# Delta rule: running sums of the log decays spread over the partitions by a DMA through DRAM instead of by matmuls

## The chip, the cores and the metric

The kernel runs on one core of one Trainium2 chip. The metric is the device time of one execution in microseconds (us). TensorE is called PE (its weight loads PEld), VectorE DVE, ScalarE ACT, GpSimdE POOL, SyncE SP. All data are float32, and a float32 matmul shows as two matmul records in the trace.

## The reference, cut to what is computed

The kernel computes four layers, each a token mixer and a feed-forward part, on an input of 8 sequences x 512 tokens x 128 channels. The change lies in the mixer of the last layer, a gated delta rule with 8 heads, keys of 128 and values of 32 channels:

```python
g = -jnp.exp(A_log)[None, None, :] * jax.nn.softplus(x @ Wa + dt_bias[None, None, :])
alpha = jnp.exp(g)
...
def step(state, inp):
    q_t, k_t, v_t, a_t, b_t = inp
    retained = jnp.einsum('bhvk,bhk->bhv', state, k_t)
    rk = retained[..., None] * k_t[:, :, None, :]
    vk = v_t[..., None] * k_t[:, :, None, :]
    state = a4 * (state - b4 * rk) + b4 * vk
    o_t = jnp.einsum('bhvk,bhk->bhv', state, q_t)
    return (state, o_t)
```

The kernel does this in chunks of 128 tokens. In a chunk, token t sees token s through exp(G_t - G_s), where G is the running sum of g from the chunk's start. So a 128 x 128 matrix of differences is needed for each head and chunk: G_t along a row, the same in all partitions, less G_s, one number for each partition.

## The kernel before, in words

`delta_rule` (L1833) works on 16 units (NU). A unit is one sequence and four of its eight heads; it has four chunks (NT) of 128 tokens, so there are 64 chunks. `all_units` writes the order of the work out by hand: `in_turn` counts turns, nine to a chunk (NI), 36 to a unit, and in each turn emits a step of `solve` (chunk n - 1 of the turn), of `make` (chunk n + 1), of `invert` (chunk n) and the pieces of preparation that `pieces_at` has put there for this and the next units. Each engine runs its own part of this list strictly in order, and waits on counting semaphores (`wait_ge`) for the others.

- `make`, part 0, in the first turn of nine, builds the decays of a chunk. PE: L2027, four matmuls, one a head. The stationary operand is g of the chunk's 128 tokens, one column repeated 128 times, the moving operand the triangle `upto3`; the result, in the PSUM bank `mk`, is G_t in every partition. DVE: L2313, four instructions, takes G_s (`gc`) from it and clips at zero, into D. Then ACT takes the exponential (L2221) and POOL masks it (L2184).
- `make`, part 1 (turn 3) and part 2 (turn 6): PE multiplies keys by queries and keys by keys (L2035, into `mk` again), DVE multiplies with D (L2318, L2323, L2326).
- `solve`, "state" (turn 0): for chunks behind the first of a unit PE applies the state (L2073, 16 records), DVE forms the right-hand side r (L2357, L2358, L2360) and scales the state (L2362). For the first chunk of a unit DVE only copies (L2353). "solve 0" (turn 1): PE, L2085, waits for r.
- `invert`: products of 32 x 32 tiles (L2042) between which ACT (L2231) or DVE (L2338, L2340) works. Its first product, in turn 1 too, waits for DVE's L2333 and L2335, which stand behind L2313 in DVE's order.
- Preparation: key taps, four accumulating matmuls a head over 512 tokens (L2133, two records each), queries (L2129), squares of the norms (POOL L2211, then PE L2141), transposes of the norms (L2145), values (L2118, L2119), small projections (L2112, in one boundary of four) and the layer norm's mean (L2106, in one of eight).
- "gate": PE forms G and the chunk's total as columns (L2152, L2153) for a whole unit at turn 6 of the unit before; DVE copies them at turn 12 (L2433 to L2436, counted as "gc"), and ACT exponentiates (L2274 to L2276). The PSUM bank is one of two that go round (`ring_bank`); `emptied` makes PE wait until the last reader of a bank is done.

SP has no work in this stage.

Of the kernel before, what the change touches and what calls it, by code (L numbers as in the profile page):

```python
# [16 lines left out]
F32 = mybir.dt.float32  # L17
U32 = mybir.dt.uint32
ALU = mybir.AluOpType
ACT = mybir.ActivationFunctionType  # L20
AX = mybir.AxisListType

C = 128
B = 8
# [87 lines left out]
def ts(i, n):  # L112
    return slice(i * n, (i + 1) * n)
# [1719 lines left out]
def delta_rule(k):  # L1833

    nc = k.nc
    TAPS, NH, NT = 4, 8, 4
    with ExitStack() as s:
# [16 lines left out]
        cv = k.sb("d_conv", [C, T], stack=s)[:]  # L1854
        S = k.sb("d_S", [C, NH, 32], stack=s)
        D = k.sb("d_D", [C, 2, 4, C], stack=s)
        A, Pm = (k.sb("d_" + n, [C, 6, 4, C], stack=s) for n in ("A", "P"))
        M = k.sb("d_M", [C, 4, 5, 4, 32], stack=s)
        A32, Y = (k.sb("d_" + n, [C, 4, 4, 32], stack=s) for n in ("A32", "Y"))
# [2 lines left out]
        P = [k.ps[:, i, :] for i in range(8)]  # L1862
        q = small

        pe, act, dve, pool, dma = k.stage("delta_start")
# [20 lines left out]
        for n in (1,):  # L1886
            pe, act, dve, pool, dma = k.stage(f"delta_taps{n}")
# [72 lines left out]
        def all_units(name):  # L1960
# [41 lines left out]
            def emptied(e, u, what, x):  # L2002


                n = ring[u, what, x] - 2
                if n < 0:
                    return
                v, was, y = order[n]
                on_dve = {("norm", 1): "nh", ("small", 0): "abread", ("gate", 2): "gc", ("out", 2): "x"}
                if (was, y) in on_dve:  # L2010
                    e.wait_ge(dve.steps, dve.at(f"u{v}" + on_dve[was, y]))
                else:
                    done = {"values": f"values{y}", "keys": f"keys{y}", "out": f"oT{y}", "norm": "nln"}[was]
                    e.wait_ge(act.steps, act.at(f"u{v}{done}"))

            with nc.Block() as block:
                @block.tensor
                def _(e):
                    def make(u, c, part):
                        n, g, t = chunk(u, c), u % 2, ts(c, C)  # L2020
                        if part == 0:
                            if c == 0:
                                e.wait_ge(dve.steps, dve.at(f"u{u}g"))
                            if (u, c) > (0, 0):
                                e.wait_ge(dve.steps, dve.at("A" + (chunk(u, c - 1) if c else chunk(u - 1, 3))))
                            for h in range(4):
                                ins = e.matmul(mk[:, ts(h, C)], q["g"][:, c, 4 * g + h:4 * g + h + 1].to_broadcast([C, C]), k.w["upto3"][:], start=True, stop=True)  # L2027
                            ins.then_inc(pe.steps, pe.did(f"gb{n}"))
                        else:
                            if c == 0 and part == 1:  # L2030
                                e.wait_ge(act.steps, act.at(f"u{u}run7"))
                            e.wait_ge(dve.steps, dve.at((f"d{n}", f"P{n}")[part - 1]))
                            for h in range(4):
                                H = 4 * (u % 3) + h
                                ins = e.matmul(mk[:, ts(h, C)], QK[:, 1, H, t], QK[:, part - 1, H, t], start=True, stop=True)  # L2035
                            ins.then_inc(pe.steps, pe.did((f"kq{n}", f"kk{n}")[part - 1]))
# [61 lines left out]
                    def prepare(u, what, x):  # L2098
# [48 lines left out]
                        elif what == "gate" and x == 2:  # L2147
# [2 lines left out]
                            emptied(e, u, "gate", 2)  # L2150
                            b = ring_bank(u, "gate", 2)
                            e.matmul(b[:, 0:16], k.w["upto3"][:], q["g"][:, :, hs], start=True, stop=True)  # L2152
                            e.matmul(b[:, 16:32], k.w["ones3"][:], q["g"][:, :, hs], start=True, stop=True).then_inc(pe.steps, pe.did(tag + "cum"))  # L2153
                        elif what == "keys":
                            emptied(e, u, "keys", x)
                            e.wait_ge(act.steps, act.at(tag + "run7"))
# [59 lines left out]
                def _(e):  # L2216
# [16 lines left out]
                    def prepare(u, what, x):  # L2233
# [29 lines left out]
                        elif what == "gate" and x == 0:  # L2263
# [5 lines left out]
                            e.activation(four("sp"), four("t"), ACT.Ln, bias=1.0).then_inc(act.steps, act.did(tag + "sp"))  # L2269
                            e.wait_ge(act.steps, act.n)  # L2270
                            e.activation(four("beta"), four("beta"), ACT.Exp, scale=-1.0).then_inc(act.steps, act.did(tag + "beta"))
                        elif what == "gate" and x == 4:
                            e.wait_ge(dve.steps, dve.at(tag + "gc"))
                            e.activation(four("ga"), four("gc"), ACT.Exp).then_inc(act.steps, act.did())  # L2274
# [26 lines left out]
                def _(e):  # L2301
# [3 lines left out]
                    def make(u, c, part):  # L2305
                        n, g = chunk(u, c), u % 2
                        a = (2 * c + g) % 6
                        if part == 0:
                            e.wait_ge(pe.steps, pe.at(f"gb{n}"))
                            if c == 0:  # L2310
                                e.wait_ge(dve.steps, dve.at(f"u{u}gc"))
                            for h in range(4):
                                e.tensor_scalar(D[:, g, h], mk[:, ts(h, C)], q["gc"][:, c, 4 * g + h:4 * g + h + 1], 0.0,  # L2313
                                                ALU.subtract, ALU.min).then_inc(dve.steps, dve.did(f"d{n}"))
                        elif part == 1:
                            e.wait_ge(pe.steps, pe.at(f"kq{n}"))
# [296 lines left out]
def build(nc, a, counts, upto=99, first=0):  # L2613
    k = Kernel(nc, counts)
    k.dram = a
    with k.stack:
        gate_rows = nc.dram_tensor("gate_rows", (8, B * T), F32).ap()
        h_rows = nc.dram_tensor("h_rows", (C, B, T), F32).ap()
        load_weights(k, a)
        if first <= 0:  # L2620
            with ExitStack() as s:
# [34 lines left out]
        with nc.Block() as block:  # L2656
            @block.sync
            def _(e):
                e.dma_start(a["out"], k.X[:]).then_inc(dma.steps, dma.did("out"))
                e.wait_ge(dma.steps, dma.at("out"))  # L2660
# [106 lines left out]
```

## Time and profile before

| | us |
|---|---|
| three runs | 4041.48, 4056.18, 4058.17 (median 4056.18) |
| span of the profiled execution | 4054.5 |
| PE busy | 3480.2 (86%) |
| DVE busy | 2420.3 (60%) |
| ACT busy | 1593.8 (39%) |
| POOL busy | 537.6 (13%) |

The delta rule's units run from about 2500 to 3964 us of the span. The page's own line on the whole span hides this stage: its engines there are read from the windows below. "PEclk" is the clock that TensorE was granted, as a share of 2.4 GHz; it is either 1.0 or 0.5 at any moment, and the share is a mean over the window. In a timeline a row is a run of like instructions, with the start of the first, the time from there to the end of the last, and in brackets how long the engine had been idle and who released it. Matmul ends are modelled and overlap the next start, so the time that a group holds PE is the distance between starts.

### The profile page before, as it was taken

The numbers are of one execution on the slowest core, as the hardware profiler recorded it, in microseconds if no ns is written. First come the engines' busy times: TensorE is split into PE (matmuls) and PEld (weight loads), VectorE is DVE, ScalarE is ACT, GpSimd is POOL, SyncE is SP. The second block draws the span as 40 slices with busy tenths as digits, with TensorE's granted clock in tenths as the row PEclk, the third lists the DMA queues.
The fourth block names the chain that finished last, engine by engine and source line by source line (L and its number), as shares of the span: only waits on it lengthen the run. The fifth ranks groups of instructions, "written<-read, shape, count | busy, mean of one in ns | idle before, by whom it ended". The sixth has DMA issues, their size and how long they took to land. (4 is left out here: it accounts for less than half of the span.)

```text
span 4054.5 us, 124079 instructions
## 1 busy us (share of the span) xinstructions
PE 3480.2 (86%) x55256; PEld 2205.5 (54%) x55256; DVE 2420.3 (60%) x6248; ACT 1593.8 (39%) x2941; POOL 537.6 (13%) x564
## 2 busy tenths in 40 slices
PE   3877777679999998899977796999999999999985
PEld 1326665225555555555556342666666666666672
DVE  3757776337777667767775112566666666666545
ACT  1653333345444444444320243444434344443323
POOL 1212222000000000000000000222222222222210
PEclk9896667789888888989765797999999999999967
DMA  2000000121111111111000001000000000000000
GB/s 88 0 0 1 1 1 1 43 72 51 47 39 36 41 36 44 41 44 34 13 3 3 16 0 44 2 3 3 3 2 2 3 3 3 3 3 3 2 3 23
DMA packets 37030, 77.12 MB, mean 19 GB/s; under 512 B 7696, under 2 KB 11153, under 8 KB 35473
## 3 DMA queue, kind: packets, MB, share of 16 engines
q1 hardware_dynamic: 36496, 69.17, 5.3%
q8 instruction: 437, 7.16, 0.7%
q14 instruction: 97, 0.79, 0.1%
HBM read 64.83 MB, written 4.33 MB: 17 GB/s over the span
## 5 line engine op out<-in xcount | busy, mean ns | idle before, releaser
L1366 PE MATMUL ps<-g_hs,g_fc 128*128 128x512 f32 x448 | 276.0, 701 | 40.9 <-ACT g_hidden L1488 22.0
L1488 ACT ACTIVATE g_hidden<-ps 128x512 f32<-128x512 f32 x224 | 133.3, 595 | 383.9 <-PE ps L1366 383.3
L2133 PE MATMUL ps<-d_hp,d_w_k 128*128 128x512 f32 x512 | 282.5, 638 | 0.0
L1257 PEld LDWEIGHTS ps<-g_Q,g_K 32*32 32x32 f32 x12288 | 193.8, 114 | 144.9 <-issue 57.3
L2211 POOL TENSOR_TENSOR d_sq<-d_QK 128x512 f32<-128x512 f32 x128 | 133.0, 1039 | 934.0 <-ACT d_QK L2262 772.7
L1257 PE MATMUL ps<-g_Q,g_K 32*32 32x32 f32 (+1 forms) x12288 | 225.1, 218 | 34.4 <-issue 10.1
L1380 PE MATMUL ps<-g_hidden,g_proj 128*128 128x512 f32 x448 | 243.0, 636 | 0.0
L2231 ACT ACTIVATE d_F<-ps 128x128 f32<-128x128 f32 x256 | 70.8, 276 | 352.9 <-PE ps L2042 349.6
L1225 POOL COPY g_xb<-X 128x512 f32<-128x512 f32 x8 | 7.3, 907 | 1232.4 <-DVE X L1686 1121.5
L2406 DVE SCALAR_TENSOR_TENSOR d_conv<-ps,w_conv_q,d_conv 128x511 f32<-128x511 f32 (+2 forms) x192 | 142.3, 741 | 34.2 <-ACT d_conv L2256 30.3
L1366 PEld LDWEIGHTS ps<-g_hs,g_fc 128*128 128x128 f32 x448 | 79.5, 210 | 149.1 <-ACT g_hidden L1488 80.5
L2189 POOL TENSOR_TENSOR d_M<-d_A,w_joins 128x128 f32<-128x128 f32 (+1 forms) x128 | 114.3, 912 | 346.3 <-ACT d_A L2225 346.3
L2042 PE MATMUL ps<-d_X,d_M 32*32 32x32 f32 x8192 | 123.2, 196 | 41.7 <-DVE d_X L2338 21.9
L1273 PE MATMUL ps<-g_V,g_KT 32*32 32x64 f32 x4096 | 136.7, 256 | 25.1 <-issue 5.4
L794 PE MATMUL ps<-att_kg,att_qx 32*128 32x96 f32 x1024 | 121.7, 355 | 41.9 <-DVE att_qx L708 27.4
L2035 PE MATMUL ps<-d_QK 128*128 128x128 f32 x1024 | 154.5, 296 | 0.0
L1380 PEld LDWEIGHTS ps<-g_hidden,g_proj 128*128 128x128 f32 x448 | 91.2, 207 | 113.5 <-issue 103.7
L2042 PEld LDWEIGHTS ps<-d_X,d_M 32*32 32x32 f32 x8192 | 95.7, 108 | 101.9 <-issue 66.0
L2365 DVE TENSOR_TENSOR d_r<-d_r,ps 32x128 f32<-32x128 f32 x192 | 55.0, 286 | 159.7 <-PE ps L2078 88.6
L1490 ACT ACTIVATE g_hidden<-g_hidden 128x512 f32<-128x512 f32 x224 | 141.1, 630 | 7.1
L794 PEld LDWEIGHTS ps<-att_kg,att_qx 32*128 32x128 f32 x1024 | 115.6, 255 | 50.9 <-DVE att_qx L708 29.5
L771 ACT ACTIVATE att_pt<-ps 96x512 f32<-96x512 f32 x128 | 75.1, 592 | 169.7 <-PE ps L811 168.6
(479 smaller groups left out, 7885.7 us busy)
## 6 DMA issues: line engine op xcount, KB each, us to landing
g_hs<-gate_rows SPq DMA_DIRECT2D x56, 256.0 KB, 3.6
g_fc<-in_c_fc_dram SPq DMA_DIRECT2D x56, 256.0 KB, 4.1
g_proj<-in_c_proj_dram SPq DMA_DIRECT2D x56, 256.0 KB, 2.8
X<-in_x_dram SPq DMA_DIRECT2D x1, 2048.0 KB, 11.0
w_c_fc<-in_c_fc_dram SPq DMA_DIRECT2D x1, 2048.0 KB, 8.0
w_c_proj<-in_c_proj_dram SPq DMA_DIRECT2D x1, 2048.0 KB, 12.4
ex_root<-gate_rows SPq DMA_DIRECT2D x1, 2048.0 KB, 15.0
h_rows<-k SPq DMA_DIRECT2D x1, 2048.0 KB, 6.3
```

Of the source, the lines that this page charges most:

```text
L794: ins = e.matmul(scored[:, g, b], qx[ts(g, 32), q, 4 * u + b, :, :].rearrange("p h q -> p (h q)"), kg[ts(g, 32), q, 4 * u + b, :], start=T ...
L1257: ins = e.matmul(later(scored, n_), keys_, queries(n_, planes, r_, 4 * i + j), start=(turn_ == 0 and part == 0 and n_ != 1), stop=(part == 1),
L1273: ins = e.matmul(P[1][ts(h4, 32), 256 + j * 64:320 + j * 64], KT[rows, (KR, KI)[part], i, ts(h4, 32)], V[rows, i, 4 * c["sg"] + h4, (slice ...
L1366: e.matmul(P[2], fc[:, n % 2, ts(f, C)], hs[:, n % 2], start=True, stop=True).then_inc(pe.steps, pe.did(now(f"u{i}")))
L1380: e.matmul(P[3], proj[:, n % 2, f, :], r[:, (16 * c["half"] + i) % 5], start=(c["half"] == 0 and i == 0), stop=(c["half"] == 1 and i == 15 ...
L1488: e.activation(r[:, slot], P[2], ACT.Relu).then_inc(act.steps, act.did(now(f"r{i}")))
L1490: e.activation(r[:, slot], r[:, slot], ACT.Square).then_inc(act.steps, act.did(now(f"q{i}")))
L2035: ins = e.matmul(mk[:, ts(h, C)], QK[:, 1, H, t], QK[:, part - 1, H, t], start=True, stop=True)
L2042: ins = e.matmul(inv[rows, h], stationary[rows, h], moving[rows, h], start=True, stop=True, tile_position=(32 * j, 32 * j))
L2133: ins = e.matmul(b, w_k[:, j, ts(H, C)], hp_of(u)[:, j:j + T], start=(j == 0), stop=(j == TAPS - 1))
L2211: e.tensor_tensor(squares(x), qk, qk, ALU.mult).then_inc(pool.steps, pool.did(f"{tag}sq{x}"))
L2406: e.scalar_tensor_tensor(cv[:, late:], tap_bank(run)[:, 0:T - late], k.w["conv_q"][:, 4 * g + run // 2, 3 - late:4 - late], cv[:, late:], ...
```

## The change

PE's four matmuls of part 0 are gone from each chunk. For a whole unit, four matmuls with a stationary operand of 4 columns (the four heads' g) form G as rows, four partitions for each chunk, at partitions 0, 32, 64 and 96 of the bank that already holds the gate sums. ACT copies them to SBUF in turn 12 (four instructions), SP writes them to DRAM in four DMAs of 2 KB, waits, waits until DVE has read the last chunk of the unit before, and reads the 8 KB back into each of 128 partitions (`wide_rows`, 1 MB). DVE's part 0 then reads SBUF instead of the PSUM bank. PE's key-query matmuls wait for the last chunk's A instead of for DVE's differences.

```diff
--- before.py
+++ after.py
@@ -1854,6 +1854,8 @@
         cv = k.sb("d_conv", [C, T], stack=s)[:]
         S = k.sb("d_S", [C, NH, 32], stack=s)
         D = k.sb("d_D", [C, 2, 4, C], stack=s)
+        row4 = k.sb("d_decay_rows", [C, C], stack=s)
+        wide_rows = k.sb("d_wide_rows", [C, 4, 4, C], stack=s)
         A, Pm = (k.sb("d_" + n, [C, 6, 4, C], stack=s) for n in ("A", "P"))
         M = k.sb("d_M", [C, 4, 5, 4, 32], stack=s)
         A32, Y = (k.sb("d_" + n, [C, 4, 4, 32], stack=s) for n in ("A32", "Y"))
@@ -2007,6 +2009,8 @@
                     return
                 v, was, y = order[n]
                 on_dve = {("norm", 1): "nh", ("small", 0): "abread", ("gate", 2): "gc", ("out", 2): "x"}
+                if (was, y) == ("gate", 2):
+                    e.wait_ge(act.steps, act.at(f"u{v}rows"))
                 if (was, y) in on_dve:
                     e.wait_ge(dve.steps, dve.at(f"u{v}" + on_dve[was, y]))
                 else:
@@ -2014,22 +2018,30 @@
                     e.wait_ge(act.steps, act.at(f"u{v}{done}"))
 
             with nc.Block() as block:
+                @block.sync
+                def _(e):
+                    for u in range(NU):
+                        e.wait_ge(act.steps, act.at(f"u{u}rows"))
+                        for j in range(NT):
+                            e.dma_start(k.gc_rows[u, ts(j, 4), :], row4[32 * j:32 * j + 4, :]).then_inc(dma.steps, dma.did(f"u{u}rows"))
+                        e.wait_ge(dma.steps, dma.at(f"u{u}rows"))
+                        if u:
+                            e.wait_ge(dve.steps, dve.at(f"d{chunk(u - 1, 3)}"))
+                        src = k.gc_rows[u:u + 1].rearrange("a r t -> a (r t)")
+                        e.dma_start(wide_rows[:].rearrange("p i h t -> p (i h t)"), src.to_broadcast([C, 16 * C])).then_inc(dma.steps, dma.did(f"u{u}wide"))
+                        e.wait_ge(dma.steps, dma.at(f"u{u}wide"))
+
                 @block.tensor
                 def _(e):
                     def make(u, c, part):
                         n, g, t = chunk(u, c), u % 2, ts(c, C)
-                        if part == 0:
-                            if c == 0:
-                                e.wait_ge(dve.steps, dve.at(f"u{u}g"))
-                            if (u, c) > (0, 0):
-                                e.wait_ge(dve.steps, dve.at("A" + (chunk(u, c - 1) if c else chunk(u - 1, 3))))
-                            for h in range(4):
-                                ins = e.matmul(mk[:, ts(h, C)], q["g"][:, c, 4 * g + h:4 * g + h + 1].to_broadcast([C, C]), k.w["upto3"][:], start=True, stop=True)
-                            ins.then_inc(pe.steps, pe.did(f"gb{n}"))
-                        else:
+                        if part:
                             if c == 0 and part == 1:
                                 e.wait_ge(act.steps, act.at(f"u{u}run7"))
-                            e.wait_ge(dve.steps, dve.at((f"d{n}", f"P{n}")[part - 1]))
+                            if part == 2:
+                                e.wait_ge(dve.steps, dve.at(f"P{n}"))
+                            elif (u, c) > (0, 0):
+                                e.wait_ge(dve.steps, dve.at("A" + (chunk(u, c - 1) if c else chunk(u - 1, 3))))
                             for h in range(4):
                                 H = 4 * (u % 3) + h
                                 ins = e.matmul(mk[:, ts(h, C)], QK[:, 1, H, t], QK[:, part - 1, H, t], start=True, stop=True)
@@ -2150,7 +2162,10 @@
                             emptied(e, u, "gate", 2)
                             b = ring_bank(u, "gate", 2)
                             e.matmul(b[:, 0:16], k.w["upto3"][:], q["g"][:, :, hs], start=True, stop=True)
-                            e.matmul(b[:, 16:32], k.w["ones3"][:], q["g"][:, :, hs], start=True, stop=True).then_inc(pe.steps, pe.did(tag + "cum"))
+                            e.matmul(b[:, 16:32], k.w["ones3"][:], q["g"][:, :, hs], start=True, stop=True)
+                            for j in range(NT):
+                                ins = e.matmul(b[32 * j:32 * j + 4, 128:256], q["g"][:, j, hs], k.w["upto3"][:], start=True, stop=True, tile_position=(0, 32 * j))
+                            ins.then_inc(pe.steps, pe.did(tag + "cum"))
                         elif what == "keys":
                             emptied(e, u, "keys", x)
                             e.wait_ge(act.steps, act.at(tag + "run7"))
@@ -2269,6 +2284,13 @@
                             e.activation(four("sp"), four("t"), ACT.Ln, bias=1.0).then_inc(act.steps, act.did(tag + "sp"))
                             e.wait_ge(act.steps, act.n)
                             e.activation(four("beta"), four("beta"), ACT.Exp, scale=-1.0).then_inc(act.steps, act.did(tag + "beta"))
+                        elif what == "gate" and x == 3:
+                            e.wait_ge(dve.steps, dve.at(tag + "gc"))
+                            if u:
+                                e.wait_ge(dma.steps, dma.at(f"u{u - 1}rows"))
+                            for j in range(NT):
+                                rows = slice(32 * j, 32 * j + 4)
+                                e.activation(row4[rows, :], ring_bank(u, "gate", 2)[rows, 128:256], ACT.Copy).then_inc(act.steps, act.did(tag + "rows"))
                         elif what == "gate" and x == 4:
                             e.wait_ge(dve.steps, dve.at(tag + "gc"))
                             e.activation(four("ga"), four("gc"), ACT.Exp).then_inc(act.steps, act.did())
@@ -2306,11 +2328,15 @@
                         n, g = chunk(u, c), u % 2
                         a = (2 * c + g) % 6
                         if part == 0:
-                            e.wait_ge(pe.steps, pe.at(f"gb{n}"))
                             if c == 0:
+                                e.wait_ge(dma.steps, dma.at(f"u{u}wide"))
                                 e.wait_ge(dve.steps, dve.at(f"u{u}gc"))
+                                if u >= 2:
+                                    e.wait_ge(dve.steps, dve.at(f"u{u - 2}ms"))
+                            else:
+                                e.wait_ge(dve.steps, dve.at("A" + chunk(u, c - 1)))
                             for h in range(4):
-                                e.tensor_scalar(D[:, g, h], mk[:, ts(h, C)], q["gc"][:, c, 4 * g + h:4 * g + h + 1], 0.0,
+                                e.tensor_scalar(D[:, g, h], wide_rows[:, c, h], q["gc"][:, c, 4 * g + h:4 * g + h + 1], 0.0,
                                                 ALU.subtract, ALU.min).then_inc(dve.steps, dve.did(f"d{n}"))
                         elif part == 1:
                             e.wait_ge(pe.steps, pe.at(f"kq{n}"))
@@ -2616,6 +2642,7 @@
     with k.stack:
         gate_rows = nc.dram_tensor("gate_rows", (8, B * T), F32).ap()
         h_rows = nc.dram_tensor("h_rows", (C, B, T), F32).ap()
+        k.gc_rows = nc.dram_tensor("gc_rows", (2 * B, 16, C), F32).ap()
         load_weights(k, a)
         if first <= 0:
             with ExitStack() as s:

```

## Rows read from the trace of the kernel before

**Rows 1.** Busy time by window: us, then PE, PEld, DVE, ACT, POOL, PEclk, DMA share, GB/s

```profile
3000.00:3100.00 100.00, 96.30 (x1865) 68.25 (x1863) 64.01 (x188) 41.97 (x92) 26.40 (x26) 1.00 0.01 3
3700.00:3800.00 100.00, 96.37 (x1861) 68.66 (x1860) 62.34 (x182) 41.01 (x93) 25.95 (x26) 0.98 0.01 3
2975.00:2980.00 5.00, 5.00 (x61) 3.05 (x60) 1.06 (x4) 1.19 (x6) 0.00 (x0) 0.72 0.00 0
```

**Rows 2.** Timeline (start, us, engine, line, shapes, count, idle before) at a chunk boundary

```profile
3053.99 1.87 PE L2073 MATMUL ps<-d_S,d_QK 128*128 128x32 f32 x16
...
3055.69 1.14 PE L2027 MATMUL ps<-w_upto,d_g 128*128 128x128 f32 x8
...
3056.48 0.29 DVE L2360 TENSOR_TENSOR d_r<-d_values_gates,d_r 128x128 f32<-128x128 f32 x1
...
3056.89 1.12 DVE L2313 TENSOR_SCALAR d_D<-ps,d_gc 128x128 f32<-128x128 f32 x4
3056.91 0.41 PE L2085 MATMUL ps<-d_r,d_Y 32*32 32x32 f32 x8
...
3057.25 1.13 PE L2133 MATMUL ps<-d_hp,d_w_k 128*128 128x512 f32 x2
...
3058.24 0.31 DVE L2335 STREAM_TRANSPOSE d_X<-d_Y 128x128 f32<-128x128 f32 x1
...
3058.70 0.45 PE L2042 MATMUL ps<-d_X,d_M 32*32 32x32 f32 x32 [0.32 <-DVE d_X L2335]
```

**Rows 3.** Timeline at a boundary where the solve's first chunk starts

```profile
3012.18 1.16 PE L2027 MATMUL ps<-w_upto,d_g 128*128 128x128 f32 x8
...
3012.39 0.16 DVE L2353 COPY d_r<-d_values_gates 128x128 f32<-128x128 f32 x1
...
3015.20 0.45 PE L2042 MATMUL ps<-d_X,d_M 32*32 32x32 f32 x32 [0.44 <-DVE d_X L2335]
```

**Rows 4.** Timeline at a boundary with another PE group behind L2027

```profile
3078.35 1.14 PE L2027 MATMUL ps<-w_upto,d_g 128*128 128x128 f32 x8
...
3081.39 1.27 POOL L2184 TENSOR_TENSOR d_D<-d_D,w_upto 128x512 f32<-128x512 f32 x1 [5.56 <-ACT d_D L2221]
...
3081.64 0.34 PEld L2042 LDWEIGHTS ps<-d_X,d_M 32*32 32x32 f32 x32 [0.76 <-issue]
```

**Rows 5.** Timeline of PE just behind the two gate-sum matmuls

```profile
3008.14 0.45 PE L2042 MATMUL ps<-d_X,d_M 32*32 32x32 f32 x31
```

**Rows 6.** Timeline of ACT and PE around the read of the gate sums

```profile
3020.74 0.21 ACT L2274 ACTIVATE d_ga<-d_gc 128x16 f32<-128x16 f32 x1 [0.64 <-DVE d_end L2436]
...
3024.31 0.10 PEld L2141 LDWEIGHTS ps<-d_sq,w_picks 128*8 128x8 f32 x2 [0.71 <-POOL d_sq L2211]
```

**Rows 7.** Groups by line on ACT (count, busy us, mean ns, idle before)

```profile
L2225 ACT ACTIVATE d_A<-d_A 32x128 f32<-32x128 f32 x256 | 78.6, 307 | 156.7 <-DVE d_A L2326 152.1
L2231 ACT ACTIVATE d_F<-ps 128x128 f32<-128x128 f32 x256 | 70.8, 276 | 352.9 <-PE ps L2042 349.6
```

**Rows 8.** Timeline of PE, stretch in which the clock fell once

```profile
2968.97 1.14 PE L2027 MATMUL ps<-w_upto,d_g 128*128 128x128 f32 x8
...
2972.43 1.05 PE L2145 MATMUL ps<-w_ident,d_square_rows 8*128 8x8 f32 x8
...
2993.18 1.03 PE L2027 MATMUL ps<-w_upto,d_g 128*128 128x128 f32 x7
```

**Rows 9.** Two lines of DVE: min/median/max ns, first and last start, form

```profile
L2399 DVE TENSOR_SCALAR d_hp<-d_OT,mod x8: 545/546/548, 2504.9 to 3656.3; 128x512 f32<-128x512 f32 x8
...
L2420 DVE TENSOR_SCALAR d_t<-d_z x16: 175/1130/1134, 2519.7 to 3784.8; 128x16 f32<-128x16 f32 x16
```

**Rows 10.** DMA issues: tile and source, KB each, us to landing

```profile
d_QK<-in_Wqk_dram SPq DMA_DIRECT2D x1, 1024.0 KB, 5.1
```

**Rows 11.** Timeline of DVE before unit 0: its sums, then L2313

```profile
2526.08 0.18 DVE L2436 TENSOR_TENSOR d_end<-d_gtot,d_gc 128x16 f32<-128x16 f32 x1
...
2543.41 0.87 DVE L2313 TENSOR_SCALAR d_D<-ps,d_gc 128x128 f32<-128x128 f32 x3 [2.23 <-PE ps L2027]
```


## The prediction, made before the changed kernel was run

> **What bounds the kernel now.** I read the windows first. In the delta stage PE is busy 96% at a granted clock of 0.98 to 1.00, DVE 62 to 64%, ACT 41%, POOL 26% [rows 1]. That looks like a stage bound by PE, in which each matmul removed comes off the time. Whether it does is decided where the matmuls stand, so I read the timeline around L2027. It has 64 boundaries in three forms, each repeated to within 0.02 us; I numbered the steps of one of each.
>
> Plain form [rows 2]: the state matmuls L2073 hold PE to 3055.69, L2027 to about 3056.65. Then L2085 (solve 0) starts only at 3056.91, because DVE's right-hand side L2360 ends at 3056.77. The key taps L2133 follow, and the first inverse product L2042 (call it f1) at 3058.70, after 0.32 us of idle, released by DVE's L2335, which ended at 3058.55. So DVE's chain behind the state, and not PE, already sets both starts. L2027 fills a hole which stays there without it. Two other forms leave more to win: where the solve starts a unit there is no state product, and the right-hand side is a copy, done at 3012.55 [rows 3]; where another PE group (L2112, or L2106) stands behind L2027, f1 waits for nobody [rows 4].
>
> **What the change removes.** Four matmuls hold PE for 0.97 to 1.09 us (starts of L2027 and of what follows, [rows 2]; its row says 1.14). Over 64 chunks that is 62 to 70 us, but only what moves f1 counts.
>
> DVE's part 0 reads SBUF now. Its four instructions take 1.12 us from PSUM [rows 2]. No row has this shape from SBUF. The nearest has 512 columns and 546 ns [rows 9], so at most 1.07 ns a column: 128 columns alone would be 0.14 us, against the 0.28 us that now lie between two of the four. Bounds: nothing saved, and 0.38 us for the four (beyond it the taps bind f1, not DVE). I take the middle of 0.14 and 0.28, 0.21 us each, 0.85 for the four and 0.27 saved, since a short instruction is mostly its fixed part.
>
> - Plain, 22 boundaries in steady running: solve 0 stays; f1 moves by DVE's 0.27 (0 to 0.38). 22 x 0.27 = 5.9.
> - Start of a unit, 15: the copy ends at 3012.55, solve 0 can start at 3012.69 (lag of 0.14 as in rows 2), the taps 0.36 later, f1 another 1.06 later: 3014.11; DVE's path, 3012.58 + 0.85 + 0.55 for the two that follow + 0.15, is 3014.13. Against 3015.20 that is 1.07 (0.79 if DVE saves nothing). 16.1.
> - With a group behind, 22 (15 and 7): solve 0 at the state's end + 1.22, as in rows 2, f1 at + 2.63 = 3080.98 instead of 3081.64: 0.66 (0.37). 14.5.
> - Six at the two ends, where other engines lead more: 0.8 each, 5.
>
> Sum of the gain: 41 us (23 to 46).
>
> **What it adds on PE.** Four matmuls a unit, four columns stationary and 128 moving, behind L2153. Above: as long as L2027's, 1.0 us. Below: 0.25, if all four run side by side, since they go to four column tiles. In rows 2, 32 records on different tiles take 0.45 us where 8 on one tile at a time take 0.41. I take 0.45, as the two records of one matmul follow each other on one tile. There is no cover: f1's successor there, L2042, starts at 3008.14 with no idle before it [rows 5]. 16 x 0.45 = 7 (4 to 16).
>
> **What it adds on ACT.** Four copies of 128 elements a unit, behind the wait for "gc", ahead of L2274 in the strict order. Behind them stand the exponentials, a table load, the SiLU of the keys; POOL squares these, and PE's L2141 already waits 0.60 us for POOL 3.57 us after L2274 [rows 6]. So what ACT loses here, PE loses. Cost of a copy: 0.17 (the distance from one L2231 to the next short instruction) below, 0.33 (a quarter of the 1.30 us that the four L2225 take in the timeline, mean 307 ns) above [rows 7]. L2225 is the nearer row: four like copies that start at partitions 0, 32, 64, 96. I take 0.28 each, 1.1 a unit, 18 us (11 to 21). PE's values matmuls also wait for these copies, as `emptied` now names them; that wait, about 0.2 us, lies inside the longer one.
>
> **DMA.** The 1 MB broadcast can be issued when DVE has read the last chunk of the unit before, which is one chunk ahead of its use: 3055.69 to 3078.35, 22 us [rows 2, 4]. The nearest load of 1 MB landed in 5.1 us [rows 10]; even twice that is covered. The four small writes end before. Before unit 0 there are 17.3 us from the sums to their use [rows 11], for both and the copies. SP has nothing else here. I price it at 0 (0 to 5 once). If the cover failed, DVE's L2313 would wait, and behind it L2333, L2335 and with them f1.
>
> So far: 41 - 7 - 18 = 16 us faster. D, exponential and mask also come earlier; nobody waits for those today, so nothing.
>
> **The clock.** A hole in PE where a group stood may cost more than its length. In steady running the clock fell five times: of the twelve windows of 100 us from 2600 to 3800 five stand below 1.00, as the second of rows 1 does, and the third catches one fall, at 0.72. Such a fall lengthened its chunk from 22.66 (rows 2 to 4) to 24.21 us [rows 8]: 1.55 us. Four of the five came behind a plain boundary, in a stretch between two taps in which PE had only f1, the transposes of 8 columns L2145 (1.05 us for eight) and 32-column products: 2.6 us without a long stream, in 15 such chunks. After the change there are 37 boundaries where, between two taps, PE has the state products of 32 columns (1.7 us), then nothing or L2112's 16 columns, then solve 0: 3.3 us with less in it. I take four such stretches in ten to bring a fall, 15 more falls at 1.55 = 23 us (bounds 0 and 37 x 1.55 = 57). This choice decides the sign.
>
> The Trainium skill (TensorE: Matmul & The Clock Gate, "Why this matters for your kernels") ties drops in the middle of a kernel to idle gaps of PE, longer ones than any here; by it nothing would fall, and the time would be the first rival's. The rows speak against it: the window at 0.72 has PE busy for all of its 5.00 us [rows 1].
>
> **A rule on the port.** DVE's L2420, a scalar operation from SBUF, takes 175 ns once and 1130 in the middle [rows 9]; it ran at 3081.56 beside POOL's L2184, 3081.39 to 3082.66 [rows 4]. So reading SBUF can cost DVE a whole POOL instruction. L2313 reads SBUF now. But POOL is the one that waits there: L2184 is released by the exponential behind L2313, after 5.56 us of idle [rows 4], so I add nothing. The Trainium skill (VectorE: DVE Perf Modes, "Mode 2×_2P") says that a float32 tensor_scalar from SBUF uses both read ports and runs at twice the rate; half of 1.07 ns for 4 x 128 columns is 0.27 us, the value taken above. The Trainium skill (GPSIMD Engine Reference, "1. Specifications") also says that POOL shares these interfaces with DVE in that mode, which speaks against the change; by rows 4 it costs nothing here, by L2420 up to 1 us a chunk, which is rival 4.
>
> **Rivals.**
> 1. The clock holds. Everything else as above: 4056 - 16 = 4040 us. For: most windows are at 1.00 now. Against: the fall in rows 8. Chance 0.29.
> 2. The slower side: nearly every one of the 37 stretches brings a fall. -16 + 57 = +41, 4097 us. It decides from about 24 falls on. For: a shorter stretch with no hole in it brings a fall four times in 15 already. Chance 0.14.
> 3. PE is the bound as its 96% says, and waits elsewhere shrink with it: -66 + 7 + 0 = 3997 us. Against: L2335's wait in rows 2. Chance 0.06.
> 4. It doesn't do what it says: the broadcast lands later than 22 us, or L2313 collides with POOL in each chunk (1 us x 64). 4056 - 16 + 64 = 4104 us. Chance 0.06.
>
> **How the numbers follow.** The sum is made against the profiled execution, whose span of 4054.5 us is 2 below the median of the runs, so I set it on 4056. Forecast, chance 0.45: 4056 - 16 + 23 = 4063 us. Without the clock the terms' bounds give -31 (46 - 4 - 11) to +14 (23 - 16 - 21) around the -16; as they don't all fall on one end I count 12 either side, and 14 for the falls (6 to 24). The range goes from 4034 (rival 1 with some more gain) to 4094 (rival 2 short of its end). A measurement of this kernel can tell 0.5% from no change, 20 us: faster is below 4036, slower above 4076. Faster: rival 3, and 0.10 of rival 1, and little of the forecast, 0.2. Slower: rivals 2 and 4 and 0.08 of the forecast, 0.28. Same: 0.52.
>
> **What would show it.** L2313 from SBUF: four in 0.85 us. Plain boundaries: solve 0 as late after the state as now, with about 1.2 us of PE idle ahead of it, put down to L2360. Start of a unit: f1 1.07 us earlier. Turn 12: PE's idle before L2141 0.60 + 1.1. New matmuls: 0.45 us a group. Broadcast: landed within 10 us, no wait for it at L2313. Granted clock: 0.93 to 0.96 in windows of 100 us instead of 0.98 to 1.00. The forecast is wrong if the clock stays at 1.00 (rival 1), if it goes below 0.90 (rival 2), or if PE shows no new idle behind L2073 (rival 3).

## The result and the profile after

Four runs of the kernel after took 4093.57 to 4118.23 us (median 4104.16), beside 4041.48 to 4077.13 (median 4057.18) for the kernel before. The ratio is 1.0119, 95% interval 1.0093 to 1.0145: 1.2% or 47 us slower, and above the range of 4034 to 4094. The profiled execution took 4104.53 us, its span 4102.6, its mean granted clock 0.849 (before 0.869). The plan's lines have moved: L2085 to L2097 (solve 0), L2133 to L2145 (key taps), L2042 to L2054 (f1 and the other inverse products), L2073 to L2085 (the state), L2141 to L2153 (squares), L2112 to L2124 (small projections), L2313 to L2339 (DVE's part 0).

The windows of the stage, against rows 1 (columns as there):

```profile
3000.00:3100.00 100.00, 93.98 (x1670) 65.19 (x1668) 57.80 (x179) 38.57 (x86) 26.66 (x26) 0.90 0.04 13
...
3700.00:3800.00 100.00, 93.98 (x1749) 64.75 (x1746) 57.95 (x173) 38.52 (x87) 23.70 (x23) 0.91 0.04 13
```

PE is still busy 94%, but at a clock of 0.90 where it had 1.00 and 0.98. What that looks like in the work is seen in PE's timeline at two plain boundaries one chunk apart, the form of rows 2:

```profile
3043.88 1.87 PE L2085 MATMUL ps<-d_S,d_QK 128*128 128x32 f32 x16
3046.80 0.60 PE L2097 MATMUL ps<-d_r,d_Y 32*32 32x32 f32 x8 [1.06 <-DVE d_r L2386]
3047.33 2.08 PE L2145 MATMUL ps<-d_hp,d_w_k 128*128 128x512 f32 x2
3049.34 0.65 PE L2054 MATMUL ps<-d_X,d_M 32*32 32x32 f32 x32
...
3067.86 1.87 PE L2085 MATMUL ps<-d_S,d_QK 128*128 128x32 f32 x16
3070.78 0.60 PE L2097 MATMUL ps<-d_r,d_Y 32*32 32x32 f32 x8 [1.06 <-DVE d_r L2386]
3071.31 2.08 PE L2145 MATMUL ps<-d_hp,d_w_k 128*128 128x512 f32 x2
3073.32 0.65 PE L2054 MATMUL ps<-d_X,d_M 32*32 32x32 f32 x32
```

Solve 0 still starts 2.92 us behind the state's start, as in rows 2, behind a hole of 1.06 us put down to DVE's right-hand side. But the tap pair behind it takes 2.08 us instead of 1.13, the next 32 products 0.65 instead of 0.45: PE runs at half its clock. The windows around the two places say for how long:

```profile
3040.00:3047.00 7.00, 5.94 (x72) 4.67 (x71) 3.27 (x13) 2.41 (x4) 4.06 (x4) 0.98 0.01 2
3048.00:3054.00 6.00, 6.00 (x87) 2.92 (x86) 1.51 (x6) 0.58 (x2) 1.26 (x1) 0.54 0.51 178
3055.00:3071.00 16.00, 14.48 (x279) 10.64 (x266) 9.29 (x28) 7.30 (x14) 3.90 (x4) 0.99 0.01 3
3072.00:3081.00 9.00, 9.00 (x100) 5.90 (x98) 2.23 (x9) 0.56 (x2) 1.26 (x1) 0.51 0.01 2
3082.00:3098.00 16.00, 15.17 (x273) 11.52 (x272) 10.25 (x30) 7.54 (x18) 3.90 (x4) 1.00 0.01 2
```

Two falls in two chunks, of about 7 and 10 us; PE is busy for every microsecond of both (6.00 of 6.00, 9.00 of 9.00). In the same way I counted, in every kernel below, the falls that begin between 2600 and 3835 us, the stage's steady part. Before: 5 falls, 20.5 us at half clock, 4.1 each. After: 27 falls, 194.6 us, 7.2 each. From the long fall with which the stage begins (it starts between 2463 and 2486 us and lasts 41 us in every kernel) to the end of the execution it is 195 us at half clock before and 375 after. Of the 27 falls, 20 stand behind the 21 plain boundaries of that stretch, 7 behind the 14 with the small projections (here L2124), and none behind the 6 with the layer norm's mean; they begin 2.6 to 5.2 us behind the start of the state products. From about 2930 us on the pattern repeats every two units, in 184.3 us where the kernel before needs 174.7 without a fall. The windows of 1200 us, before and after:

```profile
2600.00:3800.00 1200.00, 1151.05 (x21677) 816.93 (x21676) 745.06 (x2192) 487.73 (x1085) 308.51 (x300) 0.99 0.01 3
```

```profile
2600.00:3800.00 1200.00, 1124.82 (x20473) 776.80 (x20472) 690.92 (x2099) 478.20 (x1089) 295.91 (x287) 0.92 0.04 14
```

The window from 3048 to 3054 us also holds the broadcast: 178 GB/s for 6 us, 1 MB. DVE waits for no broadcast in steady running.

The other new pieces. The gate rows on PE and the copies on ACT, with what PE waits for behind them (timeline, as rows 5 and 6; SPq is SP's issue of the four small writes):

```profile
3019.32 0.40 PE L2167 MATMUL ps<-w_upto,d_g 128*4 128x128 f32 x8
...
3019.65 0.34 PE L2097 MATMUL ps<-d_r,d_Y 32*32 32x32 f32 x5
...
3031.07 1.14 ACT L2293 ACTIVATE d_decay_rows<-ps 4x128 f32<-4x128 f32 x4 [0.65 <-DVE d_end L2462]
...
3032.27 1.16 PE L2130 MATMUL ps<-d_w_v,d_hp 128*128 128x128 f32 x8 [0.16 <-ACT d_decay_rows L2293]
3032.29 1.26 SPq L2026 DMA_DIRECT2D gc_rows<-d_decay_rows  x4
...
3035.81 1.02 PE L2153 MATMUL ps<-d_sq,w_picks 128*8 128x512 f32 x2 [1.54 <-POOL d_sq L2226]
```

PE's four matmuls hold it for 0.33 us. The idle time ahead of L2153 is 1.54 us, where the same matmuls (L2141) had 0.60 in the kernel before:

```profile
3024.31 1.02 PE L2141 MATMUL ps<-d_sq,w_picks 128*8 128x512 f32 x2 [0.60 <-POOL d_sq L2211]
```

And the start of a unit, the form of rows 3:

```profile
3023.82 0.16 DVE L2379 COPY d_r<-d_values_gates 128x128 f32<-128x128 f32 x1
3023.90 0.86 DVE L2339 TENSOR_SCALAR d_D<-d_wide_rows,d_gc 128x128 f32<-128x128 f32 x4
3024.12 0.41 PE L2097 MATMUL ps<-d_r,d_Y 32*32 32x32 f32 x8
3024.46 1.12 PE L2145 MATMUL ps<-d_hp,d_w_k 128*128 128x512 f32 x2
...
3025.51 0.45 PE L2054 MATMUL ps<-d_X,d_M 32*32 32x32 f32 x32
```

f1 follows the start of the copy by 1.69 us, in rows 3 by 2.81: 1.12 us earlier. DVE's four instructions take 0.86 us.

So each piece is where the prediction has it. That leaves the clock as the suspect, which the runs had to show.

### The profile page after: what moved, and what is told of

It is laid out like the page before. It is cut to its first block and busy times, and to the rows that moved or that the text cites. A ratio compares the mean times of both kernels' runs of the same rounds, so it can differ in the third digit from the quotient of the medians.

```text
span 4102.6 us, 123485 instructions
## 1 busy us (share of the span) xinstructions
PE 3496.3 (85%) x54872; PEld 2189.7 (53%) x54872; DVE 2394.3 (58%) x6248; ACT 1607.8 (39%) x3005; POOL 537.8 (13%) x564
## 5 line engine op out<-in xcount | busy, mean ns | idle before, releaser
L2145 PE MATMUL ps<-d_hp,d_w_k 128*128 128x512 f32 x512 | 315.3, 706 | 0.0
L2047 PE MATMUL ps<-d_QK 128*128 128x128 f32 x1024 | 163.4, 308 | 0.0
L2097 PEld LDWEIGHTS ps<-d_r,d_Y 32*32 32x32 f32 x2048 | 91.0, 114 | 127.1 <-DVE d_r L2386 41.0
L794 PE MATMUL ps<-att_kg,att_qx 32*128 32x96 f32 x1024 | 121.7, 354 | 41.9 <-DVE att_qx L708 27.3
L2054 PEld LDWEIGHTS ps<-d_X,d_M 32*32 32x32 f32 x8192 | 102.5, 113 | 100.5 <-issue 67.0
L2054 PE MATMUL ps<-d_X,d_M 32*32 32x32 f32 x8192 | 131.3, 201 | 26.2 <-DVE d_X L2364 20.5
L2047 PEld LDWEIGHTS ps<-d_QK 128*128 128x128 f32 x1024 | 138.2, 210 | 23.7 <-DVE d_conv L2432 15.9
L2153 PE MATMUL ps<-d_sq,w_picks 128*8 128x512 f32 x256 | 131.2, 594 | 22.9 <-POOL d_sq L2226 22.8
```

The costliest lines, as they stand in the source:

```text
L794: ins = e.matmul(scored[:, g, b], qx[ts(g, 32), q, 4 * u + b, :, :].rearrange("p h q -> p (h q)"), kg[ts(g, 32), q, 4 * u + b, :], start=T ...
L2054: ins = e.matmul(inv[rows, h], stationary[rows, h], moving[rows, h], start=True, stop=True, tile_position=(32 * j, 32 * j))
L2145: ins = e.matmul(b, w_k[:, j, ts(H, C)], hp_of(u)[:, j:j + T], start=(j == 0), stop=(j == TAPS - 1))
L2153: e.matmul(few[0:8, :], k.w["picks"][:, row, :], squares(x), start=(x == 0), stop=(x == 7)).then_inc(pe.steps, pe.did(f"{tag}ss{x}"))
```

## The experiments

Theory A: where the matmuls stood, PE is left for some 3 us with products of 32 or fewer columns and a hole, and there the clock falls; the rest of the change is worth -16 us. Theory B: the additions cost more than summed (contention by the broadcast, ACT's copies), and the clock is a symptom. All ratios are to the kernel before, timed beside the run on the same chip. The first four experiments ran on one chip, the next four on a second, the last three on a third; the kernel before had medians of 4056.19, 4053.03 and 4058.16 us there, so that a difference of medians between two groups is less sure than one within a group. Each run's falls are those between 2600 and 3835 us of its span, and "half clock" is the time at half clock counted as above (195 us before, 375 after); both come from the one profiled execution of each kernel, which lay up to 15 us from the median of its kernel. The unread matmuls are called the fill. In the kernels made from the kernel after, lines behind the fill stand 4 further down.

### Matmuls back in the boundaries, results unread

```diff
+ if part == 0 and (u, c) > (0, 0):
+     e.wait_ge(dve.steps, dve.at("A" + <chunk before>))
+     for h in range(4):
+         e.matmul(mk[:, h * C:h * C + C], k.w["ones3"][:], k.w["upto3"][:], start=True, stop=True)
```

The kernel after, with four matmuls of the old size at each of the 63 boundaries behind the first, whose results nobody reads.

> The changed kernel, with four matmuls of the old shape (128x128 stationary, 128 columns moving) put back where the removed ones stood; nobody reads their result. Theory A (the time went into falls of TensorE's clock, which came where the matmuls are missing): the 27 falls between 2600 and 3890 us, 190 us at half clock, go back to about 5, the granted clock to 0.98 or more in windows of 100 us, and the time to 4057 + 5 (gate rows) + 15 (copies on ACT) - 6 (DVE from SBUF) = 4071 us. Theory B (the additions cost it: the broadcasts, the copies on ACT and the waits behind them): the time stays at 4104 or above.

Measured: 4053.03 us, ratio 0.9992 [0.9973, 1.0012]; 2 falls, one of them at the very end of the steady part (3832 us), half clock 174 us. The 47 us of loss are gone although every addition is there and PE does more work. It also came out 18 us under my number, which the last two experiments bear on.

Next, the same matmuls at plain boundaries only (`and (c == 0 or c == 3 and u % 2)`), where they fall into the hole:

> The changed kernel, with four unread matmuls of the old shape only in the 22 plain boundaries (PE idle 1.06 us there, the four take 0.97). Theory A: PE has no work more on its path, the 22 falls behind plain boundaries vanish, those behind a boundary with L2124 (5) stay or grow to 10: 4057 - 41 + 5 + 15 + 8 to 16 = 4044 to 4052 us, clock 0.96 or more. Theory B: 4104 us or above.

Measured: 4045.41 us, 0.9963 [0.9943, 0.9982]; 9 falls, half clock 214 us. Each of the nine stands behind a boundary with the small projections, where nothing was put back.

### The hole or the columns

The fill above closes the hole and streams columns. This one has the same place and count, but 16 moving columns instead of 128:

```diff
-     e.matmul(mk[:, h * C:h * C + C], k.w["ones3"][:], k.w["upto3"][:], ...)
+     e.matmul(mk[:, h * C:h * C + 16], k.w["ones3"][:], k.w["upto3"][:, 0:16], ...)
```

> As the one before, but the unread matmuls move 16 columns instead of 128: PE is about as long busy (weights are loaded in full), but streams an eighth of the columns. If the clock follows whether PE is idle, as a rule of the Trainium skill on the clock gate has it, the time is that of the 128-column filler, 4044 to 4052 us. If it follows what is streamed (theory A as I hold it), the falls stay: 20 or more of them, and 4095 to 4110 us.

Measured: 4090.35 us, 1.0091 [1.0059, 1.0123]; 22 falls, half clock 335 us. PE at a plain boundary, the long fill first, then the short one:

```profile
3050.12 1.87 PE L2089 MATMUL ps<-d_S,d_QK 128*128 128x32 f32 x16
3051.82 1.14 PE L2041 MATMUL ps<-w_upto,w_ones 128*128 128x128 f32 x8
3053.04 0.41 PE L2101 MATMUL ps<-d_r,d_Y 32*32 32x32 f32 x8
3053.38 1.12 PE L2149 MATMUL ps<-d_hp,d_w_k 128*128 128x512 f32 x2
```

```profile
3037.17 1.87 PE L2089 MATMUL ps<-d_S,d_QK 128*128 128x32 f32 x16
3038.87 1.04 PE L2041 MATMUL ps<-w_upto,w_ones 128*128 128x16 f32 x8
3040.09 0.60 PE L2101 MATMUL ps<-d_r,d_Y 32*32 32x32 f32 x8 [0.17 <-DVE d_r L2390]
3040.62 2.08 PE L2149 MATMUL ps<-d_hp,d_w_k 128*128 128x512 f32 x2
```

And the windows of 1200 us, long fill, then short (columns as in rows 1):

```profile
2600.00:3800.00 1200.00, 1138.76 (x21708) 795.76 (x21705) 724.04 (x2214) 502.77 (x1147) 312.80 (x303) 0.98 0.04 15
```

```profile
2600.00:3800.00 1200.00, 1141.65 (x20744) 797.34 (x20742) 694.42 (x2119) 481.61 (x1099) 298.98 (x290) 0.93 0.04 14
```

Both boundaries are full of matmuls, solve 0 stands 2.92 us behind the state in both, and PE is busy 1139 and 1142 of 1200 us. Only the one with short columns loses the clock, at the old place: 15 of its 22 falls stand behind filled boundaries, and none of the nine with long columns do. So closing the hole of 1.06 us is not enough: it was closed and the falls stayed, and what counts is what PE does there. One reservation: the ends of matmuls are modelled, so pauses within the fill can't be seen. But the weight loads of the fill take 0.97 us in both kernels, and the hole behind the short fill is 0.17 us here. By the Trainium skill (TensorE: Matmul & The Clock Gate, "Why this matters for your kernels"), which ties such drops to idle gaps, this kernel should have come out like the one with long columns. It came out 45 us slower.

### Additions and removal apart

First all additions, with the old matmuls still made and read (DVE reads the PSUM bank and waits for them as in the kernel before):

```diff
- e.tensor_scalar(D[:, g, h], wide_rows[:, c, h], ...)
+ e.wait_ge(pe.steps, pe.at(f"gb{n}"))
+ e.tensor_scalar(D[:, g, h], mk[:, ts(h, C)], ...)
```

> The changed kernel with all that it adds (gate rows, copies on ACT, writes to DRAM, 1 MB broadcast a unit, their waits), but the old four matmuls a chunk form the sums and DVE reads them from PSUM; nobody reads the broadcast. Theory A: 4057 + 5 + 15 = 4077 us at a clock of 0.98 or more. Theory B: 4104 + 6 (DVE's part is lost) = 4110 us or above.

Measured: 4091.16 us, 1.0094 [1.0061, 1.0127]; 10 falls, half clock 222 us. It is 14 us above my number, and 38 above the kernel before. In the trace two units free of falls take 177.8 us against 174.7, 1.6 a unit, 25 us for all 16, as summed. The 27 us more at half clock are worth 10 of the rest, at the price found below.

Then the removal alone: no row matmuls, no copies, no DMAs; DVE reads an SBUF tile that is filled once with -1.

```diff
+ e.memset(wide_rows[:], -1.0)
- @block.sync ... (all of it), the row matmuls, the copies, their waits
```

> Only the removal: the four matmuls a chunk are gone and DVE reads the sums from an SBUF tile that was filled once with a constant. It leaves out the gate rows, the copies on ACT, the writes and the broadcasts, so the decays are not computed. Theory A (falls of the clock, plus 25 us of additions as measured between the first runs): falls as in the changed kernel, 20 or more from 2600 to 3890 us, and 4104 - 26 = 4078 us, still slower than before. Rival B (the additions' waits, not the missing matmuls, open the holes): no more than 10 falls and 4057 - 41 = 4016 us.

Measured: 4081.7 us, 1.0074 [1.0051, 1.0098]; 36 falls, half clock 367 us. With nothing added and four matmuls a chunk less, the kernel is 0.7% slower than before. This speaks against theory B: no broadcast, no copy, and the same time at half clock (367 us, 375 after), in more and shorter falls.

The same with the four unread matmuls at plain boundaries:

> The removal alone as in the run before (decays not computed), with four unread matmuls of 128 columns in the 22 plain boundaries. Theory A: 4045 - 26 = 4019 us, 10 falls or fewer. Rival B: as without them, 4016 us, since they fit into the hole.

Measured: 4018.22 us, 0.9912 [0.9888, 0.9936]; 10 falls, half clock 194 us, as before. Again the windows of 1200 us, removal alone and with the fill:

```profile
2600.00:3800.00 1200.00, 1133.95 (x20606) 784.32 (x20605) 697.72 (x2126) 471.95 (x1053) 300.59 (x291) 0.92 0.01 2
```

```profile
2600.00:3800.00 1200.00, 1149.25 (x22067) 808.28 (x22066) 739.81 (x2256) 500.52 (x1115) 319.05 (x309) 0.99 0.01 3
```

The 92 unread matmuls (four at 23 boundaries) make the kernel 63 us faster. Pairs of kernels that differ in the fill alone give the price of the half clock: 59 us for 162 (375 less 214, after against its fill), 63 for 173 (here), 45 for 121 (short against long columns) and 54 for 139 (the lean pair below). That is 0.36, 0.37, 0.37 and 0.38 us for each us at half clock; I use 0.37. The first pair crosses two chips, and each count is of a single execution, so the agreement is closer than the data are. Two other readings give somewhat more. Two units of the kernel with short columns most often take 180.6 us with 20.5 at half clock, with long columns 173.3 with 3.4; of the removal alone 180.7 with 27.3, with its fill 170.6 with 3.4: 0.43 and 0.42. And without any edit: over 22, 24 and 27 undisturbed executions of the kernel before on the three chips, the time rises by 0.44, 0.37 and 0.41 us for each us at half clock that an execution's mean clock gives.

### A leaner way to the rows

g of a unit in 16 adjacent columns, so that one matmul gives 16 rows, one ACT copy takes them and one 8 KB write follows; with the fill at plain boundaries.

```diff
+ ins = e.matmul(b[0:16, 128:256], g16[:, g], k.w["upto3"][:], start=True, stop=True)
- for j in range(NT): ... (four matmuls, four copies, four writes)
+ e.activation(row4[0:16, :], ring_bank(u, "gate", 2)[0:16, 128:256], ACT.Copy)
+ e.dma_start(k.gc_rows[u], row4[0:16, :])
```

> The changed kernel with the gate rows made as one group: g of a unit lies in 16 adjacent columns, one matmul gives 16 rows, one copy on ACT (0.28 us instead of 1.1) and one DMA of 8 KB bring them to DRAM; and the unread matmuls of 128 columns stand in the plain boundaries. If what ACT loses PE loses, as predicted: 4045 - 16 x 0.8 = 4032 us. If ACT's copies lie beside other work: 4045 us.

Measured: 4032.16 us, 0.9948 [0.9928, 0.9967]; 15 falls, half clock 230 us. The group of its copies (duration min/median/max in ns) shows one of 266 ns a unit:

```profile
L2294 ACT ACTIVATE d_decay_rows<-ps x16: 266/266/267, 2522.9 to 3776.4; 16x128 f32<-16x128 f32 x16
```

It beats both kernels, with the reference's computation kept. Its median is 13 us below that of the version with four copies, the number expected, but the two ran on different chips: against the kernel before they are 0.52 and 0.37% faster, 6 us apart, and the intervals overlap. Surer is the comparison on its own chip, with the removal alone and its fill: 4032 against 4018 us, 14 more, of which 36 us more at half clock are 13. So at an equal clock these additions cost about 1 us, where the four-copy form costs 19 to 23 (worked out below): more is saved than the three copies.

The same without the fill:

> As the run before, without the unread matmuls. Theory A: the falls of the clock are those of the changed kernel, 4104 - 13 = 4091 us. If the four copies and four small writes were what cost the time: about 4057 us.

Measured: 4085.79 us, 1.0083 [1.0048, 1.0119]; 34 falls, half clock 369 us. That is 4 us above the removal alone (4082 us, half clock 367), again nearly nothing for the additions, and two units take 181.0 us here and 180.7 there, both with 27.3 at half clock. Without the fill the lean version too is slower than the kernel before.

Then the lean version with the fill, and two unread matmuls at the other boundaries too (`range(4 if c == 0 or c == 3 and u % 2 else 2)`):

> The kernel with the lean rows and the four unread matmuls at plain boundaries (4032 us, 15 falls, 68 us at half clock between 2600 and 3835 us), with two unread matmuls of 128 columns also at the other boundaries, where PE has the small projections or the layer norm's mean and 0.18 us of idle. Theory A (a fall needs a stretch without streaming matmuls): the falls left over stand behind just these boundaries, so some 12 of them go, about 45 us at half clock x 0.375 = 17 us; the two matmuls cost 0.57 - 0.18 = 0.4 us at 26 boundaries, 10 at most. 4025 us, 5 falls or fewer. Rival (these falls have another cause, such as the norm transposes between the taps): 4035 to 4042 us with 12 falls or more.

Measured: 4035.61 us, 0.9943 [0.9921, 0.9966]; 9 falls, half clock 205 us. Neither expectation: six falls went, not twelve, and the time didn't move. 25 us less at half clock are 9 us; the matmuls cost about the same. I had counted 26 boundaries and left out the unit starts, where PE sets f1 once DVE doesn't wait: it is 40 boundaries. The two removal-only kernels (4018 us filled at plain boundaries, 4033 filled at all) put four matmuls at those 40 at 15 us (13 by the ratios, as they ran on two chips), or 20 with 13 us less at half clock, so two of them at about 10. Three of the nine falls still stand behind the small projections, where the same kernel without them has nine, although two matmuls of 128 columns now stand there. Four stand at a place that I hadn't looked at, the output projection, where PE has transposes, 32-column products and 1.40 us of idle time:

```profile
2922.31 0.45 PE L2058 MATMUL ps<-d_X,d_M 32*32 32x32 f32 x32
2924.16 2.05 PE L2190 MATMUL ps<-d_OT,w_Wo 128*128 128x512 f32 x2 [1.40 <-ACT d_OT L2318]
```

### What the first experiment gained beyond the sum

The kernel before with only DVE's source changed (SBUF constants; PE's matmuls stay and DVE waits for them):

> The kernel before, in which VectorE's four differences read an SBUF tile of constants (-1) instead of the PSUM bank. PE's four matmuls stay, VectorE still waits for them, and nothing is added; the decays are not computed, so the output is not the reference's. It prices the source alone. By my term (0.27 us at each of 37 boundaries, 10 us): 4046 us. Rival: the kernel that keeps all matmuls was 18 us better than the sum, because reading SBUF is worth about 28 us by way of what stands behind it in VectorE's order: 4028 us. Second rival: the gain there came from VectorE no longer waiting for the matmuls, then this one is at 4050 to 4056 us.

Measured: 4043.04 us, 0.9969 [0.9952, 0.9986]; 5 falls, half clock 198 us. By the ratio 13 us, near the 10 of my term. The removal-only kernel with unread matmuls at all boundaries:

> The kernel after without everything it adds (row matmuls, copies, DMAs; the differences read constants, so the decays are not computed and the output is not the reference's), and with four unread matmuls at every boundary, as in the kernel before. Beside the run of the same kernel with the additions (4053 us) it prices the additions where the clock holds; beside the source-only kernel it prices the wait that is gone. If the additions cost 26 us here too: 4027 us. If they are cheap where the clock holds (hidden): 4040 us or more.

Measured: 4033.41 us, 0.9943 [0.9924, 0.9963]; 4 falls, half clock 181 us. The start of a unit in the source-only kernel, then in this one:

```profile
3005.66 1.16 PE L2029 MATMUL ps<-w_upto,d_g 128*128 128x128 f32 x8
...
3008.42 0.45 PE L2044 MATMUL ps<-d_X,d_M 32*32 32x32 f32 x32 [0.19 <-DVE d_X L2337]
```

```profile
2996.04 1.16 PE L2027 MATMUL ps<-w_upto,w_ones 128*128 128x128 f32 x8
...
2998.54 0.45 PE L2044 MATMUL ps<-d_X,d_M 32*32 32x32 f32 x32
```

From the matmuls to f1: 3.02 us in rows 3, 2.76 with the SBUF source, 2.50 when DVE doesn't wait for PE's results either. That second 0.26 at 15 unit starts is 4 of the 10 us between the two kernels, and 17 us less at half clock are the other 6. Beside the first experiment (4053 us) this kernel prices the additions at 20 us, 23 at an equal clock (181 against 174). So the 18 us that the first experiment was better than its sum (4057 + 5 + 15 - 6) come apart as 7 for the source (13 where the sum had 6), 4 for DVE's wait, which my expectation had left out, and 8 for 21 us less at half clock than before, less 3 for the additions (23 where the sum had 20): 16. The terms of a few us are below what one comparison can tell, and the first experiment ran on another chip than these two, so this is a plausible account and not a shown one.

## Why the prediction was wrong

**The clock, the step that failed.** The prediction named the place (the 37 boundaries without a tap) and the mechanism (a stretch of 32-column products with a hole), and the experiments confirm both, with its doubt about idle gaps; that the clock would fall there even with the hole filled by short columns it did not say. It took "four such stretches in ten" and 1.55 us a fall: 15 more falls, 23 us. There were 22 more: nearly every plain boundary had one and half of those with the small projections, where the prediction gave all the same share. That alone would be 34 us and inside the range. The larger error is the length: the 1.55 us came from one short fall (3.4 us) in the kernel before [rows 8], whereas the falls of the kernel after last up to 10 us and 7.2 on average (194.6 / 27). At 0.37 us for each us, the 180 us more at half clock (375 less 195) are 67 us. In its place then: 4057 - 16 + 67 = 4108, measured 4104; with the 0.43 found from the lengths of the units it would be 4118, so the agreement to 4 us is partly luck. Even the bound, 37 falls at 1.55, was too low at 57: I had bounded the count and not the length. What makes one fall last 3 us and the next 10 no run here took apart.

**The removal.** Predicted 41 us (23 to 46). The removal alone with the fill is 36 us (0.88%) faster than before, at the same time at half clock (194 and 195 us in the profiled executions). DVE's four from SBUF: 0.86 us for 0.85. Unit start: f1 1.12 us earlier for 1.07.

**The additions.** Predicted 25 us. With against without: 27 (both filled at plain boundaries), 22 (both unfilled), 20 (all boundaries filled); set to an equal clock 20, 19 and 23, and 25 by the lengths of the units. The three differences are of medians on different chips; by the ratios they are 21, 18 and 20. PE's rows were 0.33 us, below the 0.45 taken; ACT's copies 268 ns each, of which 0.94 us a unit arrive at PE's L2153, where 1.1 was said, and 0.16 at the values. The broadcast cost nothing that a wait shows.

**The sum without the clock.** -16. The kernel after with filled plain boundaries is 12 us faster than before with 19 us more at half clock, 7 us: -19. This part was right, and with it the forecast that the sign hangs on the clock alone.

**The rivals.** Rival 2 is what happened, with 27 falls where it put the turning point at 24 and a price per fall that was too small; it had 0.14. It deserved more: for it spoke that the kernel after has strictly less on PE in each of these stretches than the one that already fell four times in 15. Rival 4's number, 4104, was met by chance: neither of its mechanisms is in the trace. DVE does not wait for the broadcast, and the longest of the 256 L2339 takes 1058 ns, but their median is 280, and the four at a boundary take 0.86 to 0.87. Rival 1 would have been the result with the fill. Rival 3 is out: the hole is there, 1.06 us, put down to DVE. As for the ports, the prediction's estimate from the Trainium skill (VectorE: DVE Perf Modes, "Mode 2×_2P") was 0.27 us saved, and the rows gave 0.26 (1.12 less 0.86).

**What would show it.** The clock in windows of 100 us was to be 0.93 to 0.96 and came at 0.90 to 0.95; "below 0.90" was given as the sign of rival 2, and the windows stayed at 0.90 with the time at rival 2's. That line was as mis-sized as the sum.

## What to carry to other kernels

A matmul that only fills a wait on TensorE is not free to remove: before taking one out, look at what else PE streams in the few microseconds around it. Here what was left was products of 32 columns and a hole, and the clock halved behind 20 of 21 such places in steady running; where 16-column projections filled the hole, behind 7 of 14. Price such a fall by its length, not by its count (here about 0.4 us for each us at half clock), and don't take that length from the one fall at hand. If the clock does fall, unread matmuls of 128 columns in the hole can give it back: here 92 of them were worth 54 to 63 us in three kernels.

## What was not expected of the hardware

The clock fell behind boundaries in which PE shows no gap of over 0.17 us: with 16 moving columns in the fill 15 times behind filled boundaries, with 128 columns in the same time and place not once. Four fp32 copies of 4 partitions x 128 out of PSUM cost ACT 268 ns each, no less than one of 16 partitions (266), so here it paid to pack the rows before copying them. And a short fp32 tensor_scalar on DVE of 128 columns from SBUF with a scalar per partition takes 280 ns in the median, the four 0.86 us against 1.12 from PSUM [rows 2].
